# Attention and a routed expert layer on one core: the expert tiles in a deeper pipeline

## What is computed

```
# attention, 16 heads of 64, rotary embedding, causal
q, k, v = x @ Wq, x @ Wk, x @ Wv
out = softmax(causal(rope(q) rope(k)^T / 8)) v
x1  = layernorm(x + out @ Wo + bo)
# router: 8 experts, the best 2 of each token
w   = softmax(x1 @ gate_w^T + expert_bias); top_w, top_i = top_k(w, 2)
top_w = top_w / (sum(top_w) + 1e-6)
# experts, 128 -> 512 -> 128
y   = sum over the two chosen e of top_w * (gelu(x1 @ w_up[e]^T) @ w_down[e]^T)
out = layernorm(layernorm(y) + x1)
```

## Time and profile before

| | |
|---|---|
| median of the runs | 906.44 us |
| the profiled execution | 908.48 us, its span 906.7 us |
| TensorE busy | 838.4 us, 92% |
| VectorE busy | 690.5 us, 76% |
| ScalarE busy | 630.9 us, 70% |
| GpSimd busy | 531.1 us, 59% |
| mean granted TensorE clock | 0.972 of full speed |
| attention ends (last projection starts) | 698.8 us |
| expert tiles on TensorE | 702.4 to 870.8 us |
| norms and output | from there to 906.7 us |

### The profile page before, as it was taken

How to read it: one execution, slowest core, us unless ns; L and a number is a source line. 1 busy time by engine, 2 the same in 40 slices (tenths; PEclk the granted TensorE clock), 3 DMA queues, 4 the chain that set the end, 5 groups by cost and what they waited for, 6 DMA issues and landing times.

```text
span 906.7 us, 21171 instructions
## 1 busy us (share of the span) xinstructions
PE 838.4 (92%) x6238; PEld 585.6 (65%) x6238; DVE 690.5 (76%) x2845; ACT 630.9 (70%) x1681; POOL 531.1 (59%) x495
## 2 busy tenths in 40 slices
PE   7999999999999999999999999999997888889940
PEld 3556666666666666666666666666664888789830
DVE  6787887989898888989898989898887633223675
ACT  4777777787778777877877787777776464445543
POOL 4576575457655856585566657656743545545742
PEclk9999999999999999999999999999999899999975
DMA  4110110001000100010010001000122222225332
GB/s 151 37 35 31 30 42 7 19 13 51 14 24 25 37 13 27 23 39 26 15 47 14 24 14 47 16 16 19 42 65 63 61 78 70 77 60 156 112 97 70
DMA packets 51360, 40.98 MB, mean 45 GB/s; under 512 B 5936, under 2 KB 45104, under 8 KB 51248
## 3 DMA queue, kind: packets, MB, share of 16 engines
q1 hardware_dynamic: 44688, 29.59, 11.9%
q0 software_dynamic: 4352, 8.99, 3.0%
q10 hardware_dynamic: 2208, 1.06, 0.4%
HBM read 23.74 MB, written 11.67 MB: 39 GB/s over the span
## 4 chain that ended last, share of the span: by engine, by line
PE 77%; DVE 8%; issue 5%; DMA 3%; ACT 2%; POOL 2%; another core or an unknown queue 1%; SPq 0%; ACTq 0%; DVEq 0%; POOLq 0%
PE SB L695 15%; PE OB L727 15%; PE TB L714 12%; PE SB L739 7%; PE SB L864 4%; PE SB L714 3%; PE AB L684 2%; PE OB L874 2%; POOL yrows L569 2%; PE TB L874 2%; PE OB L621 1%; PE OB L622 1%; PE OB L623 1%; PE AB L685 1%; PE AB L686 1%
## 5 line engine op out<-in xcount | busy, mean ns | idle before, releaser
L938 ACT ACTIVATE Pr_all<-Sm,nmax 128x512 f32<-128x512 f32 (+3 forms) x512 | 283.1, 559 | 70.1 <-DVE nmax L1119 70.1
L1119 DVE CUSTOM_DVE_ANT_0 Sm<-SB,causal 128x512 f32<-128x512 f32 (+3 forms) x512 | 219.9, 486 | 44.8 <-PE SB L695 44.5
L462 POOL TENSOR_TENSOR shared<-shared,sin_t 128x512 f32<-128x512 f32 x63 | 80.7, 1281 | 179.7 <-DVE shared L1099 179.7
L1137 DVE SCALAR_TENSOR_TENSOR x_acc<-SB,rinv,x_acc 128x128 f32<-128x128 f32 x512 | 144.2, 345 | 39.9 <-PE SB L739 33.2
L950 ACT ACTIVATE PT<-TB 128x1024 f32<-128x1024 f32 (+2 forms) x192 | 135.1, 739 | 52.3 <-PE TB L714 52.3
L695 PE MATMUL SB<-kT,qT 64*128 64x512 f32 (+3 forms) x1024 | 166.6, 444 | 0.3 <-issue 0.3
L727 PE MATMUL OB<-PT,shared 128*64 128x128 f32 (+3 forms) x1024 | 152.8, 439 | 0.3 <-ACT PT L950 0.3
L714 PEld LDWEIGHTS TB<-ident,Pr_all 128*128 128x128 f32 x1024 | 113.8, 141 | 57.8 <-ACT Pr_all L938 49.7
L714 PE MATMUL TB<-ident,Pr_all 128*128 128x128 f32 x1024 | 136.7, 276 | 1.4 <-ACT Pr_all L938 1.4
L695 PEld LDWEIGHTS SB<-kT,qT 64*128 64x128 f32 x1024 | 77.9, 187 | 69.8 <-issue 53.3
L569 POOL DMA_INDIRECT yrows<-ys,y_row x72 | 73.1, 1015 | 69.0 <-ACT ys L1040 41.6
(11 more groups left out here) (248 smaller groups left out, 1379.7 us busy)
## 6 DMA issues: line engine op xcount, KB each, us to landing
xt<-xrows SPq DMA_DIRECT2D x72, 65.0 KB
wo<-in_wo SPq DMA_DIRECT2D x64, 64.0 KB, 1.8
PT<-yrows SPq DMA_DIRECT2D x8, 512.0 KB, 3.9
x_acc<-in_x SPq DMA_DIRECT2D x8, 256.0 KB, 3.2
wdown<-in_wdown SPq DMA_DIRECT2D x8, 256.0 KB
shared<-in_wup SPq DMA_DIRECT2D x8, 256.0 KB
out<-Pr_all SPq DMA_DIRECT2D x8, 256.0 KB, 2.3
x_next<-in_xT SPq DMA_DIRECT2D x7, 256.0 KB, 2.8
```

What stands on the lines that cost most here:

```text
L938: nc.scalar.activation(Pr[j][:, 0:n], Sm[j], ACT.Exp, bias=nmax[:, j:j + 1], scale=-1.0, accum_out=rsum[p][:, h * QB + qb:h * QB + qb + 1] ...
L1119: nc.vector.tensor_tensor_reduce(out=Sm[j], in0=SB[2 * (group % 2) + h][:, at:at + n], in1=causal[:, T - n:T], scale=-0.125, scalar=HUGE, ...
L1137: last = nc.vector.scalar_tensor_tensor(out=tile, in0=SB[2 + h][:, i * P:i * P + P], scalar=rinv[:, h * QB + i:h * QB + i + 1], in1=tile, ...
```

## The change

- TensorE's step t is now: `up` of tile t + 1, transposition of t + 3, `down` of t - 1. ScalarE's is: Gelu of t + 1, copy of t + 3, `weight_y` of t - 1. For that there are four `xT`, three `hT` (the third is `x_next`, free by then) and three banks for `up`.
- There are eight `xt` and eight `ys` (four of these lie in `OT`). SyncE loads up to eight tiles ahead.
- The early table is made inside the last units: `count_full` in unit 56, `sum_full` in unit 61, `early_places` in unit 62, `turn_places` and `write_tables` in unit 63. `transpose_x(0)` to `(2)` and `up(0)` stand around the last `attend`, ahead of the last projection. The loads of the experts' first weights begin two units earlier, with another layout of `shared`.
- `copy_rows` and `send_pad` are issued by SyncE (at its tiles 13 and 27 to 34).
- The router of the last batch is denser: places at tile 15 instead of 19, the sends at 15 to 29 instead of 19 to 33, the exponentials at 9 instead of 11.
- `load_y` stands four tiles later in SyncE's program, which itself runs four tiles further ahead.
- The square root's function table is loaded before the last two `weight_y`.

```diff
-XT = 4
+XT, GROUP = 8, 4
-FRONT_AT, FULL_AT, SUMS_AT = 0, 6, 7
+FRONT_AT, FULL_AT, SUMS_AT, EARLY_AT = 0, 0, 5, 6
+UP_AT = {58: (4,), 59: (5,), 60: (0, 1), 61: (2, 3), 62: (6, 7)}
-LAST_SEED, ... LAST_PLACE, LAST_TABLE = 1, 2, 6, 8, 10, 13, 15, 19, 21
-LAST_COPY, LAST_BEFORE = 7, 4
-LAST_SENDS = (19, 21, 23, 25, 27, 29, 31, 33)
-LAST_PADS = (22, 23, 25, 26, 28, 29, 31, 32)
+LAST_SEED, ... LAST_PLACE, LAST_TABLE = 1, 2, 6, 7, 8, 11, 13, 15, 17
+LAST_COPY, LAST_BEFORE = 13, (3, 5, 6, 10)
+LAST_SENDS = (15, 17, 19, 21, 23, 25, 27, 29)
+LAST_PADS = (27, 28, 29, 30, 31, 32, 33, 34)
...
# TensorE, behind the last unit
+            pe.wait_ge(tables_ready, 1)
+            transpose_x(0)
             attend(u, 1, PAIRS - 1)
-            turn_places(0, AB)
-            pe.wait_ge(pt_ready, 3 * u + 3)
+            pe.wait_ge(pt_ready, 3 * UNITS)
+            transpose_x(1)
+            pe.wait_ge(maxed, BLK * UNITS)
+            up(0)
+            transpose_x(2)
             pe.wait_ge(y_read, 2 * u)
             project_out(u, 1)
...
# TensorE, a tile
-                if not last:
-                    transpose_x(t + 1, (s + 1) % XT)
-                up(t, s)
+                if t + 1 < TILES:
+                    if t + 1 == 2:
+                        pe.wait_ge(y_read, 2 * UNITS)
+                    up(t + 1)
+                if t + 3 < TILES:
+                    transpose_x(t + 3)
...
# ScalarE, a tile
-                if not last:
-                    copy_xT(t + 1, s + 1)
-                act.wait_ge(up_done, t + 1)
-                nc.scalar.activation(hT[s % 2][:, :], HB[s % 2][:, :], ACT.Gelu).then_inc(gelu_done, 1)
+                if t + 1 < TILES:
+                    gelu(t + 1)
+                if t + 3 < TILES:
+                    copy_xT(t + 3)
+                if last:
+                    nc.scalar.activation(warm[:, :], eps_t[:, :], ACT.Sqrt)
                 if not first:
-                    weight_y(t - 1, (s - 1) % XT)
-                if t == LAST_COPY:
-                    copy_rows(B - 1)
-                if t in LAST_PADS:
-                    send_pad(LAST_PADS.index(t))
+                    weight_y(t - 1)
...
# SyncE, a tile
+                if t == LAST_COPY:
+                    copy_rows(B - 1)
+                if t in LAST_PADS:
+                    send_pad(LAST_PADS.index(t))
```

More of the change, by code:

```diff
@@ L83 @@
 LATE_STATS_AT, SUM_ROOT_AT = {2: 6, 5: 7}, {3: 6, 6: 7}
-AHEAD = XT - 1
-SHIFT = XT - AHEAD
+AHEAD = GROUP
 GATE_EPS = 1e-6
@@ L411, in tile_loads @@
                         load_y(b)
-            rows = [None] * XT
+            rows = [None] * GROUP
             tiles(sp, tile_loads, last_rows)
@@ L806, in attention @@
                     project_k(u + 1, *following)
+                else:
+                    turn_places(0, AB)
                 if not first:
@@ L836, in turn_places, with transpose_x, up, down @@
                 pe.wait_ge(places_ready, n + 1)
-                pe.wait_ge(k_read, UNITS)
+                if n == 0:
+                    pe.wait_ge(k_read, UNITS)
                 nc.tensor.transpose(bank[0:2, 0:P], places[:, :], ident[:, :]).then_inc(places_turned, 1)
+            def transpose_x(t):
+                pe.wait_ge(xt_in[t % XT], 16 * (t // XT + 1))
+                nc.tensor.transpose(XB[t % 2], xt[t % XT][:, 0:C], ident[:, :]).then_inc(x_tr, 1)
+            def up(t):
+                pe.wait_ge(w_ready, t + 1)
+                pe.wait_ge(xT_ready, t + 1)
+                for ib in range(IB):
+                    last = nc.tensor.matmul(HB[t % 3][:, ib * P:ib * P + P], w_tile[t % AHEAD][:, ib * P:ib * P + P], xT[t % 4][:, :],
+                                            start=True, stop=True)
+                last.then_inc(up_done, 1)
+            def down(t, e):
+                pe.wait_ge(gelu_done, t + 1)
+                wait(pe, y_ready, t - 1)
+                for ib in range(IB):
+                    last = nc.tensor.matmul(FB[t % 2], hT[t % 3][:, ib * P:ib * P + P],
+                                            wdown[:, bass.ds(e * IB + ib, 1), :].rearrange("p a c -> p (a c)"),
+                                            start=(ib == 0), stop=(ib == IB - 1))
+                last.then_inc(down_done, 1)
+            def expert(t):
+                return pe.value_load(tile_expert[0:1, bass.ds(t, 1)], min_val=0, max_val=E - 1)
             attention_units(attention)
@@ L915, in _ @@
             tiles(pe, ffn, last_tables)
-            down(TILES - 1, XT - 1, expert(TILES - 1))
+            down(TILES - 1, expert(TILES - 1))
         @block.scalar
@@ L1429, in attention @@
                         pick_second(batch - 1)
-                    if n == PLACE_AT:
+                    if n == PLACE_AT and not last:
                         place_rows(batch - 1)
@@ L1435, in attention @@
                     count_front()
+                if last:
+                    write_tables(0, AB, slice(0, EARLY))
+                    place_rows(batch - 1)
+                if not last:
+                    rope_k(u + 1)
+                if n == FULL_AT and last_batch(batch):
+                    count_full()
                 if n == SUMS_AT and last_batch(batch):
                     sum_full()
-                if not last:
-                    rope_k(u + 1)
                 for j in range(2, BLK):
@@ L1445, in attention @@
                     rope_q(u + 2)
-                if n == FULL_AT and last_batch(batch):
-                    count_full()
+                if n == EARLY_AT and last_batch(batch):
+                    early_places()
                 if batch > 0 and n == TURN_AT:
@@ L1457, in _ @@
             attention_units(attention)
-            early_places()
-            write_tables(0, AB, slice(0, EARLY))
             def take_meta(t, s):
@@ L1525, in ffn @@
                     for ahead, e in enumerate(experts(0, AHEAD)):
-                        take_expert(ahead, ahead, e)
-                if t == EARLY - XT:
+                        take_expert(ahead, e)
+                if t == EARLY - AHEAD:
                     dve.wait_ge(tables_ready, 2)
-                ending = t >= TILES - XT
-                if s == 0:
-                    next_experts[:] = experts(t + AHEAD, XT - AHEAD if ending else XT)
-                if not (ending and s >= XT - AHEAD):
-                    take_expert(t + AHEAD, (s + AHEAD) % XT, next_experts[s])
+                if t + AHEAD < TILES:
+                    if t % GROUP == 0:
+                        next_experts[:] = experts(t + AHEAD, GROUP)
+                    take_expert(t + AHEAD, next_experts[t % GROUP])
                 take_meta(t, s)
```

157 lines of the change are left out of this document (62 added, 95 removed).

## The result

| | before | after |
|---|---|---|
| time of the runs, median | 906.24 us (7 runs, 903.2 to 909.7) | 899.97 us (7 runs, 899.2 to 901.1) |
| span of the profiled execution | 906.7 us | 899.3 us |
| first `down` starts | 706.37 | 707.57 |
| last `down` starts | 869.62 | 863.43 |

What follows compares the result with a forecast made beforehand. TensorE, busy 92% of the span, bounds the kernel, so time can come only from its idle stretches or slow clock. 23.2 + 2.3 + 1.2 - 2.2 = 24.5 us off 906.4 gives 882 us, range 875 to 892.

Steps and rivals of the forecast that it cites:

- entry: Passage from attention into the expert tiles: early table, up and transpositions done in advance gain 2.3 us, bounds 0 and 4.
- tiles: Expert tiles 1 to 71: 23.2 us of waits and slow clock go, less 2.2 us for new collisions.
- 29.9 us are over: Expert tiles: 70 tiles take 162.9 us against a floor of 133.0 at 1.90 each; 23.2 of the excess should go.
- in front of a `weight_y` it sat 2.19 us: ScalarE in the expert tiles: a single stall of 2.19 us, said to fit within the deeper pipeline's slack.
- The slack of 2.5 us: Expert tiles: ScalarE may be late by some 2.5 us from the end of a step before TensorE sees it.
- the wait at step 6: Transposition of the last batch's router rows: TensorE still waits for GpSimd, 2.0 us remaining of 2.47.
- What the pipeline brings in new: Expert tiles: collisions of SyncE's in-order waits and GpSimd's sends cost 2.2 us, bounds 0 and 10.
- GpSimd's sends: Rival, expert tiles 15 to 29 and 53 to 71: sends at 1.47 us become the bound in parts; 888 us, chance 15%.
- SyncE's order: Rival, expert tiles: a wait ahead of the row loads empties the eight buffers once or twice; 886 to 891 us, chance 12%.
- the one that ended at 918 us: Rival, expert stage: GpSimd's sends set the whole pace, and denser copies make it 16 us longer; 918 us, chance 4%.
- the last rival: Expert stage doesn't deepen: first weight has only four buffers, stalls return through VectorE; 898 us, chance 6%.
- +0.4 us at the end of the attention: Units 61 to 63: sum_full (1.3 us) and early_places on a full VectorE delay the attention's end by 0.4 us, bounds 0 and 1.5.

Runs made afterwards that it cites:

- repaired: The change with sum_full called ahead of rope_k and ScalarE's copy of the rows ahead of its Gelu: 878.59 us, 0.9826 of the kernel before, on chip E.

## Why the prediction was wrong

The profiled executions, split at the first and the last `down`; a positive number is time gained. The change has one `up` and two transpositions (1.1 us) more behind it at the first `down`; they are counted to the entry.

| part | predicted | chip A (906.7 to 899.3) | chip C (890.3 to 879.3) | repaired, E, against before, C |
|---|---|---|---|---|
| entry | 2.3 | -1.2 + 1.1 = -0.1 | -0.2 + 1.1 = 0.9 | 1.9 + 1.1 = 3.0 |
| tiles | 23.2 - 2.2 = 21.0 | 163.3 - 155.9 - 1.1 = 6.3 | 146.76 - 136.82 - 1.1 = 8.8 | 9.2 |
| end | 1.2 | 37.1 - 35.9 = 1.2 | 1.3 | 1.3 |
| sum | 24.5 | 7.4 | 11.0 | 13.5 |

- **The tiles: the step that failed.** "29.9 us are over" was right, but all of it was taken to follow from the kernel's order and buffers, most of it because the rows named ScalarE. Of these, 16.4 us are absent on chip C, where no signal is late, and on chip A late signals stayed: the stage of the change takes 19.0 us more there than on C (155.9 against 136.8). The row "in front of a `weight_y` it sat 2.19 us" was such a signal (the semaphore event at 757.75, 1.85 us behind the end of the `down`), and I took it for a stall that a deeper pipeline would swallow. The two long waits of the change could not be swallowed: its slack is 2.0 us, the signals are 5.1 late.
- **The slack of 2.5 us** was mis-sized too: 2.0 measured. With 2.2 us as the commonest lateness this decides whether most of them are seen at all.
- **The kernel's own waits went as forecast**: those for sends, for rows, the ones for xT where signals are in time. The exponentials leave 0.52 (forecast 0.4), the wait at step 6 is 2.45 us on A and 1.54 on C (forecast 2.0, "stays"). Of the 13.5 us over the floor on chip C, 8.8 go and 4.7 remain, where 6.7 were to remain.
- **What the pipeline brings in new** (-2.2): nothing on chip C, where TensorE has no wait for rows or for a result bank. Neither GpSimd's sends nor SyncE's order shows in its waits on A either; these rivals fell, and so did the one that ended at 918 us. The 898 us of the last rival, the nearest number, rested on weight buffers and VectorE: VectorE does start late here, but on the same late signal as ScalarE, so its mechanism isn't what happened, and its number is near by luck.
- **The entry.** `up(2)` waits 1.26 us for VectorE (forecast 1.4) and `down(0)` follows 1.1 us behind. On this part the gain of 2.3 became 0.9 on C and nothing on A. What failed is "+0.4 us at the end of the attention": `sum_full` takes 3.4 us, not the 1.3 it took in unit 63, where GpSimd multiplies nothing. TensorE waits 2.10 us in unit 61, its clock is then down (the third number from the end of the window's row, 0.83 of full speed), and the last projection starts at 702.84, 4.1 us later than before.

```profile
673.00:683.00 10.00, 8.77 (x55) 5.37 (x57) 9.25 (x39) 7.65 (x22) 2.94 (x3) 0.83 0.19 61
```

  The price could have been read from the trace of before, where one such operation of VectorE in unit 62 takes 0.84 us and ends with GpSimd's:

```profile
681.68 0.84 DVE L1296 TENSOR_TENSOR count<-before_n,region 128x8 f32<-128x8 f32 x1
```

```profile
681.23 1.27 POOL L465 TENSOR_TENSOR kT<-shared 128x512 f32<-128x512 f32 x1
```

  The Trainium skill, page "GPSIMD Engine Reference", section "8. Key points", which the prediction cites for the sends, names VectorE's operations with two SBUF inputs; the traces agree, and I had applied it to the wrong place.
- **The end**: 1.2 forecast, 1.2 measured.

What stays open: why TensorE's signals are late on some chips. Two things on record narrow it, and neither was tested. The program has a part in where it happens: the Gelu is over 1 us late at the same 13 tiles, from 14 to 54, in the change on A and with `sum_full` ahead of `rope_k` on D (2.21 and 2.20 us at tile 14, 5.13 and 5.14 at tile 20). And the traces of A, D and F lack records: they hold 8,126 to 8,670 semaphore events, of all engines, those of B, C and E 9,911 to 10,108. So the recording of the execution may itself be part of what is slow there: every time on record comes with a traced span, and none without recording is there to compare.

## What to carry to other kernels

An idle row names the engine that released it, not who was late. Before a deeper pipeline is priced from such rows, look whether the named engine was itself free and waiting for a signal of work that had long ended; that part stays, or is a matter of the chip. Price a small operation where it will stand, with what its neighbours do there, and not where it stood; and run both kernels on a second chip before a loss is called the kernel's.

## What the runs showed of the hardware

- TensorE's completion signals can arrive late and in groups (here up to 5 us, mostly 2.2) while its products go on starting at full pace; no signal of ScalarE, VectorE or GpSimd was over 0.5 us late in the tiles. Chips A, D and F showed it, each in every kernel traced there, B, C and E in none, and then SyncE's sequencer had instructions of 0.5 to 0.7 us too (4 to 29 of them; none on the other chips). The kernel before takes 12 to 14 us more on these chips and the change 18.
- The mean granted clock differs between executions of one kernel on one chip, and the time goes with it: with `sum_full` in unit 59, 882.0 us at 0.983 and 888.8 us at 0.974. Behind the same pause of TensorE it was 1.00 in the trace of one kernel and 0.72 in that of the next, from 652 to 664 us.
- A VectorE operation with both inputs in SBUF that starts, even with 8 numbers, during a GpSimd multiplication of 1.3 us ends with it (once one that starts 0.12 us ahead, at 646.16, did too); a mask, with one input in PSUM, keeps its 0.56 us beside a multiplication (GpSimd's ran from 669.37 to 670.64 there). Four of them made 1.3 us of work last 5.5.
